# A new order for the opening of a gated linear attention block, with identity multiplies on TensorE around its first transposes

## What is computed

```python
q = elu(LN(x) @ Wq) + 1;  k = elu(LN(x) @ Wk) + 1;  v = LN(x) @ Wv      # 16 heads of 64
a = sigmoid(LN(x) @ Wa + ba + 2)                                          # one decay per head and row
# for each row, head by head:  S = a*S + k v^T;  z = a*z + k;  out = (q S) / (q z + eps)
x = x + out @ Wo
x = x + (LN(x) @ CB^T) * (SCB / 127) + bias
```

## Time and profile before

| what | value |
|---|---|
| median of 3 runs | 2088.05 us (2087.57 to 2090.41) |
| profiled execution, its own time | 2088.68 us |
| span of the profiled execution | 2086.9 us |
| PE busy | 2032.9 us (97%) |
| PEld, DVE, ACT, POOL busy | 84%, 72%, 33%, 18% |
| transfers | 220.81 MB, mean 106 GB/s |

### The profile page before, as it was taken

The page is one execution under the profiler, slowest core; times in us unless marked ns, Lnnn a source line. Parts: engine busy times, 40 slices in busy tenths (PEclk is TensorE's granted clock), DMA queues, the critical chain, the costliest instruction groups (busy, mean ns, idle before and its releaser), DMA issues. The chain is left out here.

```text
span 2086.9 us, 70847 instructions
## 1 busy us (share of the span) xinstructions
PE 2032.9 (97%) x28424; PEld 1758.7 (84%) x28424; DVE 1494.8 (72%) x2794; ACT 679.9 (33%) x1288; POOL 365.5 (18%) x368
## 2 busy tenths in 40 slices
PE   7899999999999999999999999999799999999998
PEld 5788888988888888988888889888688888888887
DVE  7677877878877787777787888777555555555555
ACT  4333343343343333433333433434211111111111
POOL 2111221322222321212321223210100000000000
PEclk9999999999999999999999999999899999999999
DMA  6233333333333333333333333342333233233332
GB/s 203 84 88 92 92 111 109 111 89 91 97 109 112 108 87 94 105 108 107 102 91 92 111 104 108 97 116 87 114 113 117 105 120 116 106 121 108 114 117 80
DMA packets 204592, 220.81 MB, mean 106 GB/s; under 512 B 31360, under 2 KB 146560, under 8 KB 204544
## 3 DMA queue, kind: packets, MB, share of 16 engines
q1 hardware_dynamic: 204544, 220.13, 34.6%
HBM read 168.59 MB, written 51.44 MB: 105 GB/s over the span
## 5 line engine op out<-in xcount | busy, mean ns | idle before, releaser
L1231 PE MATMUL G<-w_hi,xT_hi 128*128 128x512 f32 x1024 | 410.0, 400 | 4.1 <-DVE xT_lo L843 4.1
L1231 PE MATMUL G<-w_lo,xT_hi 128*128 128x512 f32 x1024 | 402.5, 393 | 0.0
L1231 PE MATMUL G<-w_hi,xT_lo 128*128 128x512 f32 x1024 | 401.1, 392 | 0.0
L703 ACT ACTIVATE relu_t<-G 128x512 f32<-128x512 f32 x256 | 153.4, 599 | 461.4 <-PE G L1231 461.4
L1231 PE MATMUL G<-xT_lo,w_hi 128*128 128x256 f32 x1024 | 289.8, 283 | 0.0
L1231 PE MATMUL G<-xT_hi,w_lo 128*128 128x256 f32 x1024 | 289.8, 283 | 0.0
L1231 PE MATMUL G<-xT_hi,w_hi 128*128 128x256 f32 x1024 | 289.7, 283 | 0.0
L1231 PEld LDWEIGHTS G<-w_hi,xT_hi 128*128 128x128 f32 x1024 | 194.1, 190 | 46.1 <-DVE xT_lo L843 4.5
L1231 PEld LDWEIGHTS G<-w_hi,xT_lo 128*128 128x128 f32 x1024 | 193.8, 189 | 42.2
L1231 PEld LDWEIGHTS G<-w_lo,xT_hi 128*128 128x128 f32 x1024 | 194.3, 190 | 36.2
L614 POOL TENSOR_TENSOR xT_in<-xT_in,bias_b 128x256 f32<-128x256 f32 x124 | 147.7, 1224 | 398.1 <-DMA bias_b<-norm_rows 398.1
(11 more groups left out here) (134 smaller groups left out, 3608.1 us busy)
## 6 DMA issues: line engine op xcount, KB each, us to landing
abc<-decay_rows SPq DMA_DIRECT2D x256, 128.0 KB, 3.1
pbc<-product_rows SPq DMA_DIRECT2D x256, 128.0 KB, 3.0
attn_rows<-attn SPq DMA_DIRECT2D x512, 64.0 KB, 2.0
at_rows<-attn_rows SPq DMA_DIRECT2D x64, 512.0 KB, 3.3
xt<-in_x SPq DMA_DIRECT2D x64, 256.0 KB, 2.9
x_in<-in_x SPq DMA_DIRECT2D x64, 256.0 KB, 3.4
out_rows<-xt SPq DMA_DIRECT2D x64, 256.0 KB, 2.0
xT_in<-in_xT SPq DMA_DIRECT2D x31, 512.0 KB, 4.2
```

Of the source, the lines that this page charges most:

```text
L703: act.activation(relu_t[buffer][:, :], bank[:, :], ACT.Relu)
L1231: made = nc.tensor.matmul(to, lhs, rhs, start=(n == 0), stop=(n == len(passes) - 1))
```

## The change

Seven edits, all in the opening:

1. SyncE issues the loads of `wa_raw` and `ba_c` behind slab 0 instead of ahead of it.
2. VectorE makes `minus_ba` and `wa` behind `x_lo(1)` instead of ahead of the moments and of the first normalisation.
3. The first half of the inputs is split ahead of slab 0 and the second half behind it, on ScalarE and on VectorE.
4. In steps -1 and 0, TensorE waits for one `lo` piece of 128 x 512 at a time, ahead of the three passes that need it, instead of for the whole slab.
5. ScalarE splits slab 4 in step 0, behind the copies of `v` and `kT`, instead of in step -1 ahead of them.
6. VectorE splits slab 5 ahead of `masked(0)` instead of behind it.
7. TensorE multiplies the identity by itself (float32, 128 x 128) into bank `G0`, six times as soon as the constants are there, and five times behind the transposes. The next product overwrites the bank.

```diff
...
         def _(sp):
             for s in range(2):
                 sp.dma_start(xt[s][:, :], x_rows[C * s:C * s + C, :]).then_inc(x_loaded[s], 16)
-            sp.dma_start(wa_raw[:, :, :], Wa.rearrange("(k p) h -> p k h", p=128)).then_inc(small_loaded, 16)
-            for c in range(2):
-                sp.dma_start(ba_c[L * c:L * c + H, :], ba.rearrange("(h a) -> h a", a=1)).then_inc(small_loaded, 16)
             for n, u in enumerate(order):
                 for kt in range(KT):
                     sp.dma_start(raw[KT * n + kt], slab(u)[:, kt, :]).then_inc(raw_loaded[n], 16)
+                if n == 0:
+                    sp.dma_start(wa_raw[:, :, :], Wa.rearrange("(k p) h -> p k h", p=128)).then_inc(small_loaded, 16)
+                    for c in range(2):
+                        sp.dma_start(ba_c[L * c:L * c + H, :], ba.rearrange("(h a) -> h a", a=1))\
+                            .then_inc(small_loaded, 16)
                 if n == 2:
                     sp.wait_ge(stats_ready, 1)
                     for s in range(2):
...
                 for kt in range(KT):
                     act.activation(w_hi[:, order[n], kt, :], raw[KT * n + kt], ACT.Copy).then_inc(w_hi_ready, 1)
 
+            first_x_hi(0)
             split_hi(0)
-            for s in range(2):
-                first_x_hi(s)
+            first_x_hi(1)
             split_hi(1)
 
...
                 if gates and not first:
                     exp_logits()
                 if second:
+                    split_hi(4)
                     split_hi(5)
                 if exists(i):
                     k1_parts()
...
                     q_parts(1)
                     if first:
                         split_hi(3)
-                        split_hi(4)
                     else:
                         chunk_decay(i, one, c32[1], c32[0])
                     copy_v(0)
...
                                             w_hi[:, order[n], kt, :].bitcast(fp32), ALU.subtract).then_inc(w_lo_ready, 1)
 
             x_stats(16)
-            dve.wait_ge(small_loaded, 48)
             dve.wait_ge(consts_ready, 1)
             dve.wait_ge(stats_ready, 1)
-            for c in range(2):
-                made = nc.vector.tensor_scalar(minus_ba[L * c:L * c + H, :], ba_c[L * c:L * c + H, :], -1.0, -SHIFT,
-                                               ALU.mult, ALU.add)
-            made.then_inc(ba_ready, 1)
             x_moments(1)
-            nc.vector.tensor_scalar(wa[:, :, 0:H], wa_raw[:, :, :], 1.0, None, ALU.mult).then_inc(wa_ready, 1)
             first_x_normal()
             for s in range(2):
                 dve.wait_ge(xnT_ready[s], 1)
                 nc.vector.tensor_scalar(xT_in[:, :, tokens(s)], tiles_of(xT_bank(s)), 1.0, None, ALU.mult)\
                     .then_inc(xT_kept, 1)
+            x_lo(0, 1, tiles_of(xT_bank(0)))
             split_lo(0)
-            for s in range(2):
-                x_lo(s, 1, tiles_of(xT_bank(s)))
+            x_lo(1, 1, tiles_of(xT_bank(1)))
+            dve.wait_ge(small_loaded, 48)
+            nc.vector.tensor_scalar(wa[:, :, 0:H], wa_raw[:, :, :], 1.0, None, ALU.mult).then_inc(wa_ready, 1)
+            for c in range(2):
+                made = nc.vector.tensor_scalar(minus_ba[L * c:L * c + H, :], ba_c[L * c:L * c + H, :], -1.0, -SHIFT,
+                                               ALU.mult, ALU.add)
+            made.then_inc(ba_ready, 1)
             split_lo(1)
 
...
                     masked(1)
                 if gates and not first:
                     x_lo(0, pairs[1], xT_in[:, :, tokens(0)])
+                if second:
+                    split_lo(5)
                 if exists(i):
                     masked(0)
                 if second:
-                    split_lo(5)
                     elu_k(1, 0)
                 if gates and not first:
                     logit_sums()
...
                                                xt[s][:, 128 * kt:128 * kt + 128], ident[:, :])
                 made.then_inc(xnT_ready[s], 1)
 
+            def warming(times):
+
+                for _ in range(times):
+                    nc.tensor.matmul(G[0][:, 0:128], ident[:, :], ident[:, :], start=True, stop=True)
+
...
...
             for stage, value in first_due.items():
                 pe.reg_mov(due_of[stage], value)
             pe.wait_ge(consts_ready, 1)
+            warming(6)
             for s in range(2):
                 transpose_x(s)
+            warming(5)
 
             def step(i, pair, b):
                 one = counts(pe, i, 1, (-2, -1, 0, 1))
...
                     if not isinstance(i, int):
                         pe.reg_alu(due_of[stage], due_of[stage], 1, ALU.add)
 
-                def product(to, passes):
+                def product(to, passes, slab_of=None):
 
                     for n, (lhs, rhs) in enumerate(passes):
+                        if starting and slab_of is not None and n % 3 == 0:
+                            pe.wait_ge(w_lo_ready, KT * order.index(slab_of) + n // 3 + 1)
                         made = nc.tensor.matmul(to, lhs, rhs, start=(n == 0), stop=(n == len(passes) - 1))
                     return made
 
                 parts = [(kt, xp, w) for kt in range(KT)
                          for xp, w in ((xT_hi, w_hi), (xT_hi, w_lo), (xT_lo, w_hi))]
 
-                def weights(slab_of):
-
-                    if starting:
-                        pe.wait_ge(w_lo_ready, KT * (order.index(slab_of) + 1))
-
                 def unit(bank, slab_of, s, ready):
 
-                    weights(slab_of)
-                    product(bank[:, :], [(xp[:, kt, tokens(s)], w[:, slab_of, kt, :]) for kt, xp, w in parts])\
+                    product(bank[:, :], [(xp[:, kt, tokens(s)], w[:, slab_of, kt, :]) for kt, xp, w in parts], slab_of)\
                         .then_inc(ready, 1)
 
                 def q_unit(bank, u):
 
-                    weights(u * QT // KT)
                     for j in range(QT):
                         t = QT * u + j
                         c = 128 * t % U
                         made = product(bank[:, 2 * C * j:2 * C * j + 2 * C],
-                                       [(w[:, 128 * t // U, kt, c:c + 128], xp[:, kt, :]) for kt, xp, w in parts])
+                                       [(w[:, 128 * t // U, kt, c:c + 128], xp[:, kt, :]) for kt, xp, w in parts],
+                                       128 * t // U)
                     made.then_inc(q_unit_ready[u], 1)
```

## The result

The changed kernel takes 2073.99 us (median of 6 runs, 2071.42 to 2075.95), the kernel before 2087.81 us (6 runs, 2083.43 to 2090.93). The ratio is 0.9936 with an interval of 0.9925 to 0.9947: 13.4 us faster, 11.1 to 15.7. I had forecast 2081.0 in a range of 2078.3 to 2085.3, so the sign was right and the forecast gain, 7.1 us, was half of the measured one. No figure in this document uses two executions that took nearly twice as long as the others: 3979.1 us in experiment 2, and 3980.93 us of the kernel before beside experiments 5 to 8.

What follows compares the result with a forecast made beforehand. The loop was taken as bound by TensorE. Head 3.9, idleness 2.1, clock 2.1 and rounding 0.2, less 1.2 for `pbc`, gave 7.1 us: from 2088.68 to 2081.6, or 2081.0 as median, range 2078.3 to 2085.3.

Steps and rivals of the forecast that it cites:

- The sum: Opening to `v0_unit` of step 0: gains less the new wait make 7.1 us.
- Head: Opening up to `v0_unit` of step -1: it starts at 21.8 instead of 25.74 us, a gain of 3.9.
- The clock: At the first product, about 11.9 us: TensorE's clock already high, its matmuls 0.24 us apart instead of 0.42.
- Edit 5's terms: Around `scores`: 2.1 us less TensorE idleness ahead, and 2.1 us because the clock stays high behind.
- the new wait for `pbc`: Ahead of `v0_unit` of step 0, at 43.5 us: TensorE waits about 1 us, taken as 1.2 off the gain.
- theory A: Code supply: TensorE's waits behind the opening belong to fetching its own program; 44 added instructions move them, giving half the gain.
- B: Behind the opening, everything merely runs earlier and meets the transfers otherwise; 2076 us expected without the identity multiplies.
- C: The difference behind the opening is the scatter of the runs; 2080 us expected without the identity multiplies.
- The clock still low at the first product: First product at 0.42 us a matmul, everything behind up to 2.1 us later: gain 5.0, 2083.1 us; chance 15%.
- Gaps without a visible releaser take some back: TensorE's four `delta` gaps, 8.9 us: two more clock falls, gain 3.7, 2084.4; without the one fall, 8.8; chance 12%.
- Another engine takes it back: Steps 0 and 1: the chain of broadcasts keeps its old time, the total ends at 2087 us; chance 9%.
- slower: `delta` gaps all become 3.6 us with three more clock falls: 3.5 us slower, 2091.6; chance 4%.

Runs made afterwards that it cites:

- experiment 2: Changed kernel with eleven one-column multiplies in place of its eleven identity multiplies: ratio 0.9950, median 2079.09 us.
- experiments 5 to 8: Kernel before with 64 (0.9994) or 22 (0.9996) one-column multiplies; changed kernel with slab 4 split early again (0.9962) or waiting for whole slabs again (0.9965).
- experiment 7: Changed kernel with slab 4 split early again, in step -1 ahead of the copies of `v` and `kT`: ratio 0.9962, median 2079.64 us.
- experiment 4: Kernel before with eleven one-column multiplies ahead of the transposes and nothing else: ratio 0.9981, median 2082.26 us.
- experiment 1: Changed kernel without its eleven identity multiplies, the other six edits kept: ratio 0.9984, median 2083.52 us.
- the eight kernels: The changed kernel and seven variants, all with 44 machine instructions moved against the kernel before; their waits between 50 and 160 us total 5.6 to 7.2 us.
- experiment 11: Changed kernel with the five identity multiplies behind the transposes replaced by five one-column ones: ratio 0.9952, median 2079.16 us.
- experiment 8: Changed kernel with TensorE waiting for whole slabs again instead of single `lo` pieces: ratio 0.9965, median 2080.59 us.
- experiment 3: Kernel before with only the eleven identity multiplies added, six ahead of the transposes and five behind: ratio 0.9958, median 2080.23 us.
- experiment 12: Changed kernel with VectorE making `masked(0)` ahead of slab 5's `lo` pieces again: ratio 0.9939, median 2076.38 us.
- experiment 9: Changed kernel with two identity multiplies behind the transposes instead of five, 32 machine instructions moved: ratio 0.9951, median 2079.55 us.

## Why the prediction was half right

**The opening: right but for one term.** The sum said 7.1 us by `v0_unit` of step 0; it is 8.0 there (50.65 to 42.62) and 7.7 at the transposes of step 1. Head 3.9 forecast, 3.91 measured. The clock: high from 11.91 on. The float32 multiply of the identity takes 0.45 ahead of the transposes (six from 5.21 to 7.93), near the 0.44 built from the transposes. Edit 5's terms (2.1 idle time and 2.1 clock) were 3.4 together at `delta(0)` by experiment 7 (36.07 against 32.67) and 2.7 at step 1, as the changed kernel's small waits for slab 5 and `pbc` take up a part. The one term over-sized was the new wait for `pbc`, 1.2 in the sum: it measured 0.20. VectorE was done with `qs` at 37.7 and not 38.45. State and `qs` took 1.93 us instead of the 2.74 of before; there they ran beside GpSimd's pass over `xT_in` (40.59 to 49.25), in the changed kernel they were through ahead of it (from 37.88). That nothing else shortened them is not shown.

**The step that failed** is a term that the sum doesn't contain: what the moved code does to TensorE's waits in steps 1 to 4. I priced the eleven multiplies by the work they hide behind, let the sum end at `v0_unit` of step 0, and put everything behind it at nothing ("time won ahead of it stays won"). The waits without a releaser came in only as a rival that costs ("the added instructions and the shift change what these gaps fall on. They can also shrink"), with 12% and at most 1.7 us of gain. That rival also counted only the four gaps in `delta`, 8.9 us, of such waits. Measured, the steps 1 to 4 took 4.1 us less (99.8 to 95.6) as these waits went from 10.1 to 5.6 us. In the timings, moving the code alone is worth 4.0 us (1.3 to 6.9) in experiment 4, and 4.4 by the medians or 7 by the ratios between experiments 1 and 2. The opening's 7.7 and these 4.1 make 11.8 of the 13.4; the other 1.6 us lie within the interval of the measurement. The mechanism is theory A. B fell with experiments 1 and 4: in the first, everything ran 5.7 us earlier with the waits at the old places, in the second 0.7 us earlier with the waits at new ones. C fell with experiment 3, and with the eight kernels that repeat the same places.

**What is shown and what is argued.** Shown is that the places of the waits move with the number of instructions ahead of them, return with 256, and that the waits end shortly behind a packet of the instruction queue. That TensorE waits for its own code there is inferred from this; 256 instructions would fill the 16 KB of one packet (0.57 MB in 35) if an instruction has 64 bytes, which no trace shows. What decides when a packet moves, and so why the waits are 5.6 at one place and 9.8 at another, stays open, and no run separates it from the transfers beside it. Open too is the scatter of the loop: single steps that take 21.59 us at best take up to 22.30 in the kernel before and 22.42 in the changed one, in changing iterations.

**The rivals.** *The clock still low at the first product*: did not happen, but it was near: with five fewer real multiplies (experiment 11) or a start at 13.7 (experiment 8) the clock falls inside the product. The Trainium skill (TensorE: Matmul & The Clock Gate, Part 4) has it that transposes don't count as activity. Experiment 11 fits: its six multiplies are followed by transposes and 1.75 us of rest, and the clock falls; it does not prove the rule. *Gaps without a visible releaser take some back*: the right place to look, with the wrong sign. *Another engine takes it back* and *slower*: no trace of either.

## What to carry to other kernels

Lay out an opening from unit prices and lags between engines, as here: it met every mark of TensorE named above within 0.5 us, but the last (42.62 for 43.5). But in a long written-out program like this one, an edit that adds or removes TensorE instructions can also move and resize waits that no other engine causes, here by 4.1 us in four steps: look for idle time without a releaser, count the machine instructions that an edit adds, and separate the two effects by a twin that adds as many and does nothing. Where an idle engine is kept busy for its clock, keep it so until just ahead of the real work (here 1.3 us of idleness was harmless and 1.75 was not).

## What the runs showed of the hardware

- The waits without a releaser have a period in TensorE's code: 256 machine instructions more brought back a wait of 3.58 us in the same product of step 2, with 10 of 32 records left instead of 11. With 44 more, it stands 22 records earlier.
- Such a wait ends 2.1 to 3.9 us behind the last packet of the instruction queue (59 waits in fourteen profiles).
- A clock that has risen fell again inside the product that followed 1.75 us of idleness behind six multiplies and eight transposes (experiment 11), also after 1.98 us (experiment 8) and 2.39 (experiment 3), but not after 1.28 (experiment 12), 1.22 (experiment 9) or 0.69 us.
- Early in the span the granted clock of the profile can read 1.00 while matmuls run at the low pace (14 to 18 us before: 1.00, 0.42 us apart).
- Executions of one kernel scatter by up to 14 us (2073.01 to 2086.84 in experiment 7).
